# A fused attention and feed-forward block on one core: another order of the same steps on TensorE

## What is computed

```
x = x + layernorm(attn(layernorm(x)))
x = x + layernorm(ffn(layernorm(x)))

attn:  q, k, v = split(h @ Wqkv.T + b)          # 8 pairs of query heads, 4 of key heads
       p1, p2  = softmax(causal(q_m @ k_m.T * D**-0.5)), m = 0, 1
       lam     = exp(sum(lq1*lk1)) - exp(sum(lq2*lk2)) + lambda_init
       o       = (p1 - lam * p2) @ v             # per head pair, 256 wide
       o       = o * rsqrt(mean(o*o) + eps) * subln_w * (1 - lambda_init)
       return o @ out_w.T + out_b
ffn:   h = hadamard(h * SU_ug) / 64
       h = silu(h @ W_gate.T * scale) * (h @ W_up.T * scale)
       return hadamard(h * SU_dp) / 64 @ W_down.T * scale
```

## Time and profile before

| | us |
|---|---|
| median of three runs | 1370.04 |
| lowest, highest | 1369.92, 1370.52 |
| the profiled execution | 1370.52 |
| its span | 1368.7 |
| TensorE busy | 1351.8 (99%) |
| VectorE busy | 1026.2 (75%) |
| ScalarE busy | 888.6 (65%) |
| GpSimd busy | 868.3 (63%) |

### The profile page before, as it was taken

How to read it: one execution, slowest core, us unless ns; L and a number is a source line. 1 busy time by engine, 2 the same in 40 slices (tenths; PEclk the granted TensorE clock), 3 DMA queues, 4 the chain that set the end, 5 groups by cost and what they waited for, 6 DMA issues and landing times.

```text
span 1368.7 us, 26497 instructions
## 1 busy us (share of the span) xinstructions
PE 1351.8 (99%) x8342; PEld 1206.2 (88%) x8342; DVE 1026.2 (75%) x2589; ACT 888.6 (65%) x2494; POOL 868.3 (63%) x1352
## 2 busy tenths in 40 slices
...
DMA packets 9752, 18.50 MB, mean 14 GB/s; under 512 B 912, under 2 KB 7312, under 8 KB 9104
## 3 DMA queue, kind: packets, MB, share of 16 engines
...
...
## 4 chain that ended last, share of the span: by engine, by line
PE 86%; DVE 6%; POOL 4%; ACT 2%; issue 2%; DMA 1%; SPq 0%; ACTq 0%; POOLq 0%; DVEq 0%
PE turn_bank L720 9%; PE score_bank L698 8%; PE score_bank L700 8%; PE score_bank L699 8%; PE score_bank L815 7%; PE turn_bank L722 5%; PE sum_bank L720 5%; PE turn_bank L707 4%; PE proj_bank L720 3%; PE proj_bank L766 3%; PE turn_bank L780 3%; PE sum_bank L722 2%; PE turn_bank L766 2%; PE sum_bank L707 2%; PE proj_bank L780 2%; PE proj_bank L707 2%
## 5 line engine op out<-in xcount | busy, mean ns | idle before, releaser
L850 ACT ACTIVATE e<-score_bank,negmx 128x512 f32<-128x512 f32 (+2 forms) x640 | 395.0, 627 | 85.8 <-DVE negmx L1068 84.5
L1313 POOL TENSOR_TENSOR e<-e,e 128x512 f32<-128x512 f32 (+3 forms) x256 | 294.7, 1151 | 21.4
L1064 DVE TENSOR_REDUCE mx<-score_bank 128x1 f32<-128x512 f32 (+1 forms) x384 | 242.1, 638 | 41.4 <-PE score_bank L700 40.0
L698 PE MATMUL score_bank<-k_hi,q_hi 128*128 128x512 f32 (+2 forms) x640 | 258.7, 404 | 2.7 <-ACT e L850 2.2
L1296 POOL TENSOR_TENSOR inv_s<-s,neg_one 128x1 f32<-128x1 f32 x128 | 70.6, 551 | 280.8 <-DVE s L1280 280.7
L720 PE MATMUL turn_bank<-v_hl,pT_hi 128*128 128x512 f32 x633 | 230.2, 398 | 1.8 <-DVE pT_lo L1074 1.3
L700 PE MATMUL score_bank<-k_hi,q_lo 128*128 128x512 f32 (+2 forms) x640 | 231.5, 362 | 0.0
L699 PE MATMUL score_bank<-k_lo,q_hi 128*128 128x512 f32 (+2 forms) x640 | 231.2, 361 | 0.0
L1310 POOL TENSOR_SCALAR e<-e,ratio 128x512 f32<-128x512 f32 (+3 forms) x256 | 181.2, 708 | 12.0
L1059 DVE CUSTOM_DVE_ANT_0 score_bank<-score_bank,mask 128x384 f32<-128x384 f32 (+3 forms) x256 | 143.4, 560 | 50.2 <-PE score_bank L700 48.7
L722 PE MATMUL turn_bank<-v_hl,pT_lo 128*128 128x256 f32 x633 | 177.4, 280 | 0.0
...
## 6 DMA issues: line engine op xcount, KB each, us to landing
...
```

Source lines behind the costliest of these rows:

```text
L698: pe.matmul(bank[:, 0:w], qh, kh, start=True, stop=False)
L850: act.activation(e, S[k % NS][:, 0:w], ACT.Exp, bias=negmx[:, d % 2, m, s:s + 1], accum_out=ssum[:, d % 4, s, m, c:c + 1]).then_inc(s_act, 1)
L1064: dve.tensor_reduce(mx[:, d % 2, m, s, c:c + 1], S[k % NS][:, 0:w], X, ALU.max)\
L1313: pool.tensor_tensor(a, a, b, ALU.add).then_inc(p_pool, 1)
```

## The change

The change replaces the tables of the order: FIRST_STEPS, HALVES, HEAD, TURN_OF_GROUP, LAST_GROUP, WITH_GATED, LAST_HALVES and both tables of lags. No step is added or taken away, but the first idle block has 32 matmuls in place of 38. Two waits are written differently in the code, as the order of the steps that they cover has changed: TensorE's QP waits for the transposed x in `u == 0` only, and ScalarE's first K with `g == 0 and m == 0 and c == 0` waits for the columns. Two lines of each larger table stand for the rest:

```diff
-HALVES = ('TSTTTSSSPoTSQTOPPP', 'STSTSOTTTSPSoQPPP')
+HALVES = ('STSTSSTTPSToTQPPPO', 'STSTSSOTPTSoQPPPT')
-    3: 'TQSKSTPSSSP', 4: 'TSSVTSSTTPSoQPPTOTP', 5: 'TVSTSPOTSQSSoTPVPPT'}
+    3: 'TSQKSTSVSPSP', 4: 'TSSTSSTPTSoTQPPPOT', 5: 'TSSTVSOSTPSoTQPTPVP'}
...
 FIRST_STEPS = (
-    ("LN", 0), ("LN", 1), ("NX", 0), ("WK", 0), ("NX", 1), ("IDLE", 38), ("X", 0), ("X", 1), ("IDLE", 8),
+    ("LN", 0), ("LN", 1), ("IDLE", 32), ("NX", 0), ("WK", 0), ("NX", 1), ("X", 0), ("X", 1), ("IDLE", 8),
...
-    ("S", (0, 0, 1)), ("K", (0, 1, 1)), ("LN", 3), ("WO", (0, 1)), ("QP", (0, 0, 0)), ("K", (0, 1, 2)),
-    ("K", (0, 0, 2)), ("S", (0, 0, 2)), ("NX", 3), ("WO", (0, 0)), ("S", (0, 0, 3)), ("QP", (0, 0, 1)),
-    ("V", (0, 0)), ("X", 6), ("S", (0, 0, 4)), ("X", 7), ("V", (0, 1)), ("S", (0, 1, 0)), ("S", (0, 1, 1)),
-    ("LAM", None), ("S", (0, 1, 2)), ("S", (0, 1, 3)), ("S", (0, 1, 4)), ("QP", (1, 1, 0)), ("K", (0, 1, 3)),
-    ("S", (1, 0, 0)), ("V", (0, 2)), ("QP", (1, 0, 0)), ("S", (1, 0, 1)), ("V", (0, 3)), ("V", (0, 4)),
-    ("S", (1, 0, 2)), ("S", (1, 0, 3)), ("S", (1, 0, 4)), ("QP", (1, 0, 1)))
+    ("S", (0, 0, 1)), ("K", (0, 1, 1)), ("LN", 3), ("WO", (0, 1)), ("QP", (0, 0, 0)), ("K", (0, 0, 2)),
+    ("S", (0, 0, 2)), ("WO", (0, 0)), ("K", (0, 1, 2)), ("NX", 3), ("S", (0, 0, 3)), ("S", (0, 0, 4)),
+    ("QP", (0, 0, 1)), ("LAM", None), ("V", (0, 0)), ("X", 6), ("X", 7), ("S", (0, 1, 0)), ("V", (0, 1)),
+    ("S", (0, 1, 1)), ("V", (0, 2)), ("S", (0, 1, 2)), ("K", (0, 1, 3)), ("S", (0, 1, 3)), ("S", (0, 1, 4)),
+    ("S", (1, 0, 0)), ("QP", (1, 0, 0)), ("S", (1, 0, 1)), ("V", (0, 3)), ("V", (0, 4)), ("S", (1, 0, 2)),
+    ("S", (1, 0, 3)), ("QP", (1, 1, 0)), ("S", (1, 0, 4)), ("QP", (1, 0, 1)))
...
 SCALAR_LAGS = {
-    "K": 1, "V": 1, "QP": 0, "OP": 0, ("K", (0, 0, 1)): 0, ("K", (0, 1, 1)): 0, ("K", (0, 1, 3)): 0,
-    ("NX", 2): 2, ("QP", (0, 1, 1)): 1, ("V", (0, 0)): 2, ("V", (0, 3)): 2, ("V", (0, 4)): 2, ("WQ", 0): 1,
-    ("X", 1): 1, ("X", 3): 3, ("X", 7): 1}
+    "K": 1, "V": 1, "QP": 0, "OP": 0, ("K", (0, 0, 1)): 0, ("V", (0, 1)): 2}
...
-                        if u < 2:
+                        if u == 0:
                             pe.wait_ge(t_lo, t_use["X", CT * ((tok + HID - 1) // BANK) + 1] + 1)
...
-                        if kv_use[kind, what] == 0:
+                        if g == 0 and m == 0 and c == 0:
                             act.wait_ge(cols_landed, 16)
```

23 lines of the change are left out of this document (12 added, 11 removed), and 21 rows, old and new, of tables (FIRST_STEPS, VECTOR_LAGS, WITH_GATED).

## The result

The changed kernel takes 1381.18 us (median; 1380.62 to 1382.54), the kernel before 1370.14 beside it: the ratio is 1.0081, 95% interval 1.0065 to 1.0095. It is slower by 11 us. The prediction said 1369.7 and gave slower a chance of 0.20. The profiled execution took 1379.9 with a span of 1378.1, 9.4 above that of before. It was the quickest execution of the changed kernel, so about 1.6 us of the 11 are in no trace.

What follows compares the result with a forecast made beforehand. TensorE's own work was taken as the floor, with about 25 us of stalls movable; 0+1.0+0.9-2.2 = -0.3 us gave 1370.2 profiled, 1369.7 as median, own range 1367.6 to 1372.2, overall range 1366.0 to 1373.8.

Steps and rivals of the forecast that it cites:

- Start: Idle block before X0: six fewer idle matmuls give 0, covered by the wait for x_in; without that cover -0.65 us.
- rival 4: Longer pause before X0 drops the granted clock to 1.2 GHz; some 3 us lost, 1373; chance 0.03.
- Head, +1.0: 15 to 60 us: three new waits of 0.8, 0.7 and 1.3 less 1.8 of old ones; between -1.1 and +2.6.
- S(0,0,2) with 0.8: Head: S(0,0,2), one K nearer to QP(0,0,0), was to wait 0.8 us for its q_lo.
- 0.7 and 1.3 for two steps: Head: lambda instructions moved ahead on VectorE delay K(0,1,3) by 0.7 us and S(1,0,1) by 1.3.
- Groups 0 to 2, +0.9: Three times -0.53+0.40+0.25+0.30, rounded to +1.3 us, less 0.4 at duo 17; between -1.5 and +4.
- the gain of 2.0 us for the ratio's waits: Groups 0 to 2: duo 5's wait, 0.53 us three times, and 0.4 for pT_lo behind duo 17's turns were to go.
- Last group, -2.2: Last group and tail: gains at OP96 (1.45), PV(48,1) (0.63), PV(61,4) (0.45), small ones; new waits 0.7; between -4 and +0.5.
- The Hadamard stretch: 980 to 995 us, losing 0.84 us with GpSimd busy for 13.28 of 15; same GpSimd work, so left unchanged.
- Of the small ones 0.4 go. New: 0.7: Last group: 0.4 us of small waits go; S(54,0,2), T(55,1) behind F0 and PV(50,3) lose 0.7 together.
- Rival 2: Turns of duos, groups 0 to 2: GpSimd-blocked mix falls ahead of a reduce or pT_lo, 5.4 us over the sum; 1374; chance 0.16.
- Rival 1: Last group's gain stands alone: groups -0.7, head 0, tail -2.7 us, giving 1366.6; chance 0.25.

Runs made afterwards that it cites:

- the lag: VectorE's mixes put one step later, nothing else moved: 1375.64 us in the changed kernel, 1364.99 us in the kernel before.
- the run with longer mixes and 5 us less: The kernel before with VectorE's mixes one step later, nothing else: 1364.99 us against 1369.95, ratio 0.9965.

## Why the prediction was wrong

- **Start.** Right: X0 starts at 9.23 with 32 idle matmuls and 9.34 with 38. The pause before it grew by more than the 0.65 us of the prediction, by 1.6: by starts it is 1.9 us, before 0.3. The clock stood, so rival 4 falls: the granted clock stays at 1.00, and the eight idle matmuls behind X1 take 1.04 us as before. TensorE's first groups by line:

```profile
2.05 5.49 PE L670 MATMUL score_bank<-ident 128*128 128x128 f32 x32 [2.05 <-POOL ident L1330]
...
9.23 0.55 PE L677 MATMUL turn_bank<-ident,x_in 128*128 128x128 f32 x3 [1.69 <-ACT x_in L907]
```

The 1.69 us before X0 are put down to ScalarE's x_in, the cover that the prediction named.

- **Head, +1.0.** The sum came out near (1.2 measured by itself), and S(0,0,2) with 0.8 exactly, but in part by luck. S(1,0,1) waits 1.5 us where I had put 0.7 and 1.3 for two steps, and the mechanism was another: k_lo ahead of the mask reduce, not lambda. K(0,1,3) waits for nothing, and K(0,0,3), which I did not name, for 0.5.
- **Groups 0 to 2, +0.9: the first step that failed.** The table has 6.0 us. Three of the terms held or nearly: duo 5's wait went, PV(2,3) waits 0.42+0.11 for my 0.40, and S(14,0,1) has 0.5 more for my 0.30. What failed is the gain of 2.0 us for the ratio's waits, duo 5's three times and 0.4 at duo 17: I went through the waits that before had and the turns that I had suspected, and booked these as gone. At duo 17 PV(17,0) still waits 0.31 of its 0.41, and at duo 5 the wait moved: QP(4,0,0) 0.34 in each group, QP(10,0,0) about 0.5 and QP(10,1,1) about 0.4 in two. By starts the ratio's waits in the groups went from 2.5 to 3.5 us, +1.0 in place of -2.0, and in the whole kernel the mixes wait 10.1 us in place of 6.7. That is 3.0 of the 5.1 us that the step is off. Most of the rest is some ten waits of 0.1 us in each group, 2.0 us in all, at turns whose cover had been just enough; I had 0.25 a group for three of them. Against the kernel before the ratio makes only this 1.0 of the 6.0, which is why the lag did not bring the two kernels together.
- **Last group, -2.2: the second step that failed.** By the table it is +3.3. The first part was right: 2.4 us are gained up to S(50,1,4), at OP96 and PV(48,1), OP96 with no wait left where I had kept 0.45. The Hadamard stretch, which I left at nothing, takes 0.8 of it back. "Of the small ones 0.4 go. New: 0.7" failed: from S(56,0,4) on the waits grow from 5.8 to 10.5 us. S(59,0,4) with 1.99, S(60,1,4) 1.65, T(55,1) 0.83 and F0 0.69 were all new, and of these I had only T(55,1). I had looked at the mix ahead of a mask reduce where it went (duo 5), not where the new strings put it (duo 59). The norm steps, which WITH_GATED's and LAST_GROUP's strings move, I had not priced at all, though each is 1.0 us of GpSimd, 1.1 to 2 us of ScalarE and up to 2 of VectorE put ahead of something: S(60,1,4) and F0 hang on them, as the runs show that moved them.
- **Rival 2** had the right sign and the right place, a mix ahead of a pT_lo, but not the mechanism: the mix there waited for the ratio, while the time with which mixes overlap GpSimd did not decide, as the run with longer mixes and 5 us less shows. It named 1374, and 1381 was measured. **Rival 1** takes 0.7 us for duo 5 and duo 17, where my own terms give 2.0, so its 1366.6 should have been 1365.3; the result is far from either.
- **The range.** My error was one of method: existing waits were counted as what can be lost, and 25 us of stalls as the scale. A new order has no such ceiling. Looking back, slower should have had more than 0.20, as many covers were changed at once, while only a few large waits could be gained.
